# A gated expert layer's opening: the last context and the shared expert's weights loaded between the first tiles' rows, and a low part of context 1 behind the normalization chain of tiles 1 and 2

## What is computed

```python
# expert of a token: min(clip(id, 0, 24999) // 6250, 3); ids are drawn from 13 to 99985
g = silu(einsum('bsd,fd->bsf', h, ctx[e])); u = einsum('bsd,fd->bsf', h, ctx[e])
y = einsum('bsf,df->bsd', g * u, ctx[e])           # kept where the token's expert is e
x = x + tanh(g_xattn) * layer1(layernorm(x))
# layer 2: top 2 of 16 by sqrt(softplus(logits)) + bias, capacity 256 for each expert,
# W1, W3 (352 x 512), W2 (512 x 352); shared expert Ws1, Ws3, Ws2 for every token
x = x + tanh(g_ffn) * layer2(layernorm(x))
```

## Time and profile before

| | |
|---|---|
| median of 3 runs | 484.9 us (484.44 to 484.98) |
| the profiled execution | 489.42 us |
| its span, first to last instruction | 487.6 us |
| TensorE busy | 463.7 us, 95% of the span |
| VectorE busy | 328.8 us, 67% |
| ScalarE busy | 256.4 us, 53% |
| GpSimd busy | 209.9 us, 43% |
| mean granted clock of TensorE | 0.989 |

### The profile page before, as it was taken

The page is one execution under the profiler, slowest core; times in us unless marked ns, Lnnn a source line. Parts: engine busy times, 40 slices in busy tenths (PEclk is TensorE's granted clock), DMA queues, the critical chain, the costliest instruction groups (busy, mean ns, idle before and its releaser), DMA issues.

```text
span 487.6 us, 7790 instructions
## 1 busy us (share of the span) xinstructions
PE 463.7 (95%) x2493; PEld 394.6 (81%) x2493; DVE 328.8 (67%) x724; ACT 256.4 (53%) x379; POOL 209.9 (43%) x175
## 2 busy tenths in 40 slices
PE   2879999999999998999999999999999999999993
PEld 1358877888888876888888999999999999999982
DVE  6549988998896834388747776666666666666520
ACT  4834444555554334472344576666666666666531
POOL 0601444555544264452456625444435544442242
PEclk9979999999999999999999999999999999999998
DMA  7825654666756353261539999988869988887545
GB/s 291 283 72 185 205 173 153 195 238 221 253 189 223 108 155 134 71 79 28 76 103 223 251 299 292 279 261 236 260 230 237 281 265 252 259 265 230 109 60 70
DMA packets 29164, 95.02 MB, mean 195 GB/s; under 512 B 4816, under 2 KB 5328, under 8 KB 28624
## 3 DMA queue, kind: packets, MB, share of 16 engines
q0 software_dynamic: 17040, 43.66, 36.5%
q1 hardware_dynamic: 11808, 50.98, 30.4%
q10 hardware_dynamic: 288, 0.01, 0.0%
HBM read 67.50 MB, written 28.70 MB: 197 GB/s over the span
## 4 chain that ended last, share of the span: by engine, by line
PE 85%; DVE 6%; DMA 2%; issue 2%; ACT 1%; POOL 1%; POOLq 0%; another core or an unknown queue 0%; DVEq 0%
PE psG L1275 47%; PE psY L1275 29%; PE psT L1280 6%; DMA ys<-in_x,idx 2%; PE psG L1521 1%; DMA tok_i<-in_ids 1%; DVE xh_sb L903 1%; PE psY L1292 1%; DVE arena L912 1%; DVE arena L908 1%; DVE stats L937 0%; DVE stats L930 0%; DVE gu L919 0%; POOL front L419 0%; POOLq L81 0%
## 5 line engine op out<-in xcount | busy, mean ns | idle before, releaser
L1275 PE MATMUL psY<-arena 128*128 (+1 forms) x372 | 92.2, 398 | 0.0
L1275 PEld LDWEIGHTS psY<-arena 128*128 128x128 f32 x372 | 68.0, 188 | 13.7
L1275 PE MATMUL psG<-arena 128*128 x228 | 59.8, 413 | 4.7 <-DVE arena L912 4.7
L498 POOL DMA_INDIRECT ht<-out,idx x32 | 33.7, 1053 | 65.0 <-PE psT L1280 49.2
L1275 PE MATMUL psY<-slot,arena 128*128 128x512 f32 x240 | 58.9, 395 | 0.0
L1050 DVE TENSOR_TENSOR slot<-raw,slot 128x1536 fp32r<-128x1536 f32 x25 | 43.9, 1757 | 19.7 <-ACT slot L622 18.9
L1275 PEld LDWEIGHTS psG<-arena 128*128 128x128 f32 x228 | 43.2, 195 | 15.0 <-issue 6.5
L1050 DVE TENSOR_TENSOR arena<-raw,arena 128x1536 fp32r<-128x1536 f32 x24 | 42.0, 1757 | 17.2 <-ACT arena L622 17.1
L1275 PEld LDWEIGHTS psY<-slot,arena 128*128 128x128 f32 x240 | 44.2, 188 | 9.4 <-ACT xh_sb L666 0.2
L1275 PE MATMUL psG<-arena,slot 128*128 128x512 f32 x216 | 51.3, 392 | 0.0
L1275 PEld LDWEIGHTS psG<-arena,slot 128*128 128x128 f32 x216 | 40.1, 188 | 8.2
(11 more groups left out here) (228 smaller groups left out, 806.3 us busy)
## 6 DMA issues: line engine op xcount, KB each, us to landing
raw<-in_w SPq DMA_DIRECT2D x51, 768.0 KB
padded<-xh_sb SPq DMA_DIRECT2D x19, 256.0 KB
raw<-in_ctx_t SPq DMA_DIRECT2D x2, 1024.0 KB, 8.7
ht<-in_ctx_t SPq DMA_DIRECT2D x1, 1024.0 KB, 11.6
xh_sb<-in_ctx_t SPq DMA_DIRECT2D x1, 1024.0 KB
out<-log_sb SPq DMA_DIRECT2D x4, 256.0 KB
ht<-out,idx POOLq DMA_INDIRECT x32
xb<-in_x,idx POOLq DMA_INDIRECT x19
```

Of the source, the lines that this page charges most:

```text
L498: pool.indirect_dma_start(ht[:, n, :], None, halves_of_out, slots(e * NA + a, 0)).then_inc(g_here[n], 16)
L1275: ins = pe.matmul(ps, left[a], right[b], start=n == 0 and m == 0, stop=n == total - 1 and m == 2)
```

## The change

It has four parts.

1. SyncE: context 3, the bias and the zeros wait for tile 2's rows (xa_here[2]) in place of first_out. The three loads of the shared expert's weights are no longer issued together ahead of all padded rows, but one behind each of the padded rows of tiles 1, 2 and 3.
2. VectorE: low_ctx(1) goes from ahead of the first statistics to the end of the pair's step, behind its Newton chain. The two halves of low_ctx(3) go from steps 0 and 1 to steps 1 and 2; behind the first VectorE waits for its completion, behind the second for the count of 4.
3. ScalarE: high_ctx(3) goes from step -1 to step 1, between the copy of the transposed gates and the silu. take_rest(2, 1) goes from step -2 to step -1.
4. TensorE: rest(2, 1) goes from ahead of the first step to step -1, behind the transposes of h(0), in front of rest(2, 2).

```diff
--- before.py
+++ after.py
@@ -361,19 +361,19 @@
             for e in range(E1 - 1):
                 sp.dma_start(ctx_raw(e), ctx_t[e, :, :]).then_inc(ctx_here[e], 16)
 
-            sp.wait_ge(first_out, 1)
+            sp.wait_ge(xa_here[2], 16)
             sp.dma_start(ctx_raw(E1 - 1), ctx_t[E1 - 1, :, :]).then_inc(ctx_here[E1 - 1], 16)
             sp.dma_start(bias_b[:, :], gate_b).then_inc(in_bias, 16)
             sp.wait_ge(zeroed, 1)
             for a, b in ((a, b) for a in range(NA) for b in range(2)):
                 sp.dma_start(out[TOK + a * P:TOK + (a + 1) * P, b * D:(b + 1) * D], zeros[:, :]).then_inc(spare_sent, 16)
-            sp.wait_ge(ctx_lo_done, E1)
-            for c in range(3):
-                load(0, c)
-
             for t in range(NT):
                 sp.wait_ge(xh_ready, t + 1)
                 sp.dma_start(padded[t * P:(t + 1) * P, :], xh_sb[:, t % 2, D:2 * D]).then_inc(padded_sent[t % 2], 16)
+                if 1 <= t < 4:
+
+                    sp.wait_ge(ctx_lo_done, E1)
+                    load(0, t - 1)
 
 
             sp.wait_ge(bT_ps, NJ)
@@ -573,6 +573,8 @@
                 if have(known, -1):
                     act.wait_ge(gT_ps, t)
                     act.activation(gT[0], psT[1][:, :], ACT.Copy).then_inc(gT_hi, 1)
+                if known == 1:
+                    high_ctx(3)
                 if known == NT:
                     silu(0)
                     copy_logits(0)
@@ -591,9 +593,10 @@
                     act.wait_ge(hT_ps, t + 2)
                     act.activation(hT[0], psT[0][:, :], ACT.Copy).then_inc(hT_hi, 1)
                 if known == -1:
-                    high_ctx(3)
-                if known in (-1, 0):
-                    take_rest(2, known + 3)
+                    take_rest(2, 1)
+                    take_rest(2, 2)
+                if known == 0:
+                    take_rest(2, 3)
                 act.wait_ge(norm_ready, t + 3)
                 if have(known, 2):
                     if had(known, 1):
@@ -601,7 +604,6 @@
                     norm(h[:, par, :], xa_of(t, par, known), 1 if known == 0 else 0, h_ready)
                 if known == FIRST:
                     take_rest(2, 0)
-                    take_rest(2, 1)
                 if have(known, -2):
                     norm(xh_sb[:, par, D:2 * D], xh_sb[:, par, 0:D], 1, xh_ready)
                 if known in (SPLIT, SPLIT + 1):
@@ -878,9 +880,6 @@
             link(dve.scalar_tensor_tensor(past[1], iota[:, 0:NT], S(14)[:, 2:3], past[0], ALU.is_ge, ALU.add))
             dve.scalar_tensor_tensor(tile_e[:, :], iota[:, 0:NT], S(14)[:, 3:4], past[1],
                                      ALU.is_ge, ALU.add).then_inc(tile_ready, 1)
-
-            dve.wait_ge(first_out, 1)
-            link(low_ctx(1, 0, 1))
             dve.wait_ge(tg_ready, 1)
 
 
@@ -970,9 +969,6 @@
                             nw(dve.scalar_tensor_tensor(Y, T, -((27 / 4 * RS_W) ** (1 / 3)), Y, ALU.add, ALU.mult))
                             if pair:
                                 low_h()
-
-                                dve.wait_ge(ctx_lo_done, 1)
-                                dve.nop(nofuse=True).then_inc(ctx_lo_done, 1)
                     nw(dve.scalar_tensor_tensor(T, T, -10 / 3 * RS_W, T, ALU.add, ALU.mult))
                     if had(known, 2):
                         dve.wait_ge(h_ready, t + 2)
@@ -985,12 +981,18 @@
                     gate1()
                 if have(known, 1) and known not in (FIRST + 1, 0):
                     low_h()
-                if known in (0, 1):
-                    if known:
+                if pair:
+
+                    dve.wait_ge(ctx_lo_done, 1)
+                    low_ctx(1, 0, 1).then_inc(ctx_lo_done, 1)
+                if known in (1, 2):
+                    if known == 2:
                         dve.wait_ge(ctx_lo_done, 3)
-                    i = low_ctx(3, known, 2)
-                    if known:
-                        i.then_inc(ctx_lo_done, 1)
+                        low_ctx(3, 1, 2).then_inc(ctx_lo_done, 1)
+
+                        dve.wait_ge(ctx_lo_done, E1)
+                    else:
+                        link(low_ctx(3, 0, 2))
                 if known in (3, 4):
                     rank_digits(known - 3)
                 if known in (5, 6):
@@ -1308,7 +1310,6 @@
             for i in range(KD):
                 rest(0, i)
             rest(2, 0)
-            rest(2, 1)
             pe.wait_ge(rest_taken, KD)
             pe.wait_ge(tile_ready, 1)
             pe.nop(nofuse=True)
@@ -1346,8 +1347,11 @@
                 if have(known, 1):
                     pe.wait_ge(h_ready, t + 2)
                     transpose4(psT[0], h[:, (par + 1) % 2, :]).then_inc(hT_ps, 1)
-                if known in (-1, 0):
-                    rest(2, known + 3)
+                if known == -1:
+                    rest(2, 1)
+                    rest(2, 2)
+                if known == 0:
+                    rest(2, 3)
                 if ROWS0 <= known < ROWS0 + TB:
                     transposed(known - ROWS0)
                 if known == NT - 1:
```

## The result

| | before | after |
|---|---|---|
| median of 20 runs each | 485.22 us (483.97 to 487.69) | 483.33 us (481.6 to 484.96) |
| ratio | | 0.9958, 95% interval 0.9948 to 0.9969 |
| the profiled execution | 489.42 us | 483.97 us |
| its span | 487.6 us | 482.2 us |
| mean granted clock | 0.989 | 0.996 |

The change makes the kernel 1.9 us faster; 5.4 were forecast, and 483.33 lies outside the range. The two profiled executions do differ by 5.4 us. That this is the forecast number is luck, as the experiments show: some 3.5 us of it have nothing to do with the change.

What follows compares the result with a forecast made beforehand. Bound: in the opening TensorE idles for tile 2's rows, then runs at half clock; later VectorE's unbroken chain. Terms -3.74 - 2.45 - 0.2 + 0.96 = -5.4 us took 484.9 to 479.5 us, range 478.4 to 482.2.

Steps and rivals of the forecast that it cites:

- The opening: Before tile 1's product: tile 2's rows land near 19.2 us without 2 MB beside them; tile 1's product 6.4 us earlier.
- Rival 1: Opening: tile 2's rows come only half as much earlier, at 21.7 us; first product 24.7, total 480.6; chance 12%.
- The rule of turns: DMA engines serve queue rows round robin, packet by packet; by this alone the gain would be some 1.1 us smaller.
- The clock: TensorE in the opening: without idling, the clock stays high; first product 3.03 us instead of 5.48, 2.45 us gained.
- ScalarE's and the moved pieces: Context 3's high part in step 1 costs under 0.1 us; context 2's low piece, moved behind tile 0's transposes, some 0.4.
- VectorE's lag: Half of context 3's low part, new in step 2, makes VectorE 0.96 us late in step 3, with nothing absorbed.
- The three loads: Shared expert's loads, one a step behind padded rows of tiles 1 to 3: cost 0, at most 3 x 0.5 us.
- The prediction's own sign: The prediction is wrong if VectorE waits for a transfer between steps 3 and 7.
- Rival 4: Steps 4 to 7: loads between rows delay gathers and scatters, VectorE waits up to 2 us; 481 to 482; chance 7%.
- The sum: Whole kernel: -3.74 - 2.45 - 0.2 + 0.96 = -5.4 us, from 484.9 to 479.5 us.

Runs made afterwards that it cites:

- before_spread: The kernel before with only the shared expert's three loads moved between the padded rows: 488.37 us, ratio 1.0068.
- after_again: The changed kernel run once more, nothing changed: 483.42 us against 485.19 for the kernel before, ratio 0.9965.
- before_again: The kernel before, unchanged, profiled once more, on the second chip: profiled execution 490.51 us; the kernel before's median there is 489.78.
- burst_early_again: burst_early unchanged, run again on the second chip: 485.24 us against 489.78 for the kernel before, ratio 0.9906.
- early_ctx3_first: burst_early with context 3, bias and zeros released by first_out again, as before the change: 483.77 us, ratio 0.9962.
- burst_early: The changed kernel with the shared expert's three loads in one burst ahead of all padded rows, at count 2: 479.94 us, ratio 0.9902.

## Why the prediction was wrong, point by point

- *The opening.* Forecast: first product at 23.55 for 3.03 us, tile 1's at 28.7, 6.4 us gained. Measured: 23.17, 2.91, 28.17; on one chip 34.84 to 28.41 (before_spread and after_again), 6.4 us, and on the other 34.73 to 28.41 (before_again and burst_early_again, which has the same opening), 6.3. Right in size and mostly in cause. The cause was incomplete: I put the lateness of tile 2's rows wholly on the 2 MB beside them, and read the gather's 1.85 us as part of that. By early_ctx3_first against the old order, 2.4 to 2.7 us of tile 1's product (34.73 or 35.08 to 32.34) came from the rest of the change, where context 1's low part had held up GpSimd; the volume was worth 4.0 (32.34 to 28.30). Rival 1 didn't come: tile 2's gather landed 3.7 us after its start. The rule of turns named there gives no reason for it, either, since it tells how transfers share while both run, and the 2 MB no longer stood beside the rows.
- *The clock.* Forecast: stays at the upper level. Measured: 1.00 from 26.9 to 33.3 us, where it had been 0.50. (In the earlier trace rows the last slice stands at 8, besides the third at 7; the forecast passes over it, and nothing rests on it.)
- *ScalarE's and the moved pieces.* Context 3's high part waited for nothing, as forecast; the rest piece costs 0.4 us at the first product (23.27 to 22.87 without it), as forecast.
- *VectorE's lag.* Forecast 0.96 us, not absorbed. x1 of tile 1 came 1.03 us later against tile 0's (7.28 in place of 6.25). At tile 18's product 0.94 and 0.68 were measured on the two chips, as a difference that holds whatever else changed there; of work added in the same place 0.85 of 1.26 us stayed. So the size is about right, and "not absorbed" holds for two thirds.
- *The three loads.* **This is the step that failed:** "The rows' scatter that x1 needs two steps on has roughly 5 us, and one load's 2.3 us beside it fits. Cost: 0; bound from above 3 x 0.5 us." Measured: 3.7 us by the changed kernel against burst_early (116.52 against 112.82 us from tile 1's to tile 18's product, both on the first chip) and 3.5 by the times. The room was even larger than stated (issue of the scatter to x1, 61.03 - 55.11 = 5.9 us before). What was wrong is the price of the load: it was taken as its bytes divided by the full rate, 2.3 us, and no landing of a scatter was read. Measured, a load issued just ahead lengthened the scatters by 5.1, 4.3 and 3.8 us (8.1, 8.0 and 7.1 in place of 3.0, 3.7 and 3.3), and 8.1 doesn't fit in 5.9. The prediction's own sign for this, VectorE waiting for a transfer between steps 3 and 7, came. Rival 4 had the mechanism and the place, with 7% and up to 2 us.
- *The sum.* -5.4 + 3.7 = -1.7, measured -1.9 and -1.8. The size of each part is a difference of single traces, so the agreement to 0.2 us says no more than that no large part is missing.

Why the first piece costs 2.3 us, the second nothing and the third 1.3 to 1.6 can be worked out. In burst_early, where nothing waits, the time from the scatter's issue to x1 is 5.9, 6.3 and 5.7 us (49.22 to 55.14, 55.70 to 61.99, 62.72 to 68.43). Against landings of 8.1, 8.0 and 7.1 this leaves 2.2, 1.7 and 1.4 us; and the second is covered, because VectorE then runs 2.3 us late from the first wait: x1 of tile 4 came at 64.20, and the scatter issued at 55.55 had landed near 63.6.

Not settled: why a load of 2.3 us at full rate lengthens a scatter by 4 to 5. From 48.6 to 57.2 us, while the first of them was under way, the share of the DMA engines was 0.77, so they weren't full all the time.

## What to carry to other kernels

A load that nobody waits for is not free: what it delays are the transfers issued beside it, so look for the one with the least room, and measure that one's landing, before calling a load hidden. The best place for a bulk load is a stretch in which the DMA engines idle, once its buffer is free: here a wait for the count that the buffer needs (2), not for the last one (4), gave 479.9 us. Check whether two traces come from the same kind of execution before reading their difference as the change's: here some 3.5 of 5.4 us were not.

## What the runs showed of the hardware

A GpSimd gather that begins while VectorE subtracts two fp32 operands in SBUF is held up till VectorE is done: it took 1.62 to 3.00 us instead of 0.95, ending 0.8 us behind VectorE each time. One that began 0.01 us behind VectorE's operation, or ahead of it, was not (0.99 us). From the other side, a 128 x 1 VectorE operation with two inputs in SBUF took 2.31 us instead of 0.16 beside a GpSimd subtraction and ended with it; that was seen once. A scatter of a tile's rows (512 KB) took 3.0 to 4.4 us from issue to landing, and 6.8 to 8.2 with a load of 768 KB issued 0.4 to 0.5 us ahead of it. A 256 KB write behind three such loads in SyncE's own queue landed after 11.2 us instead of 2.2. The same program took 485.2 us on one chip and 489.8 on another.
